# Delta rule: sums of squares of q and k by 32-column ones matmuls and selector matmuls

## The reference, cut to what matters

```python
mixed = jax.nn.silu(conv)
q, k, v = jnp.split(mixed, [KEY_DIM, 2 * KEY_DIM], axis=-1)
...
l2n = lambda t: t / jnp.maximum(jnp.linalg.norm(t, axis=-1, keepdims=True), 1e-12)
q, k = (l2n(q), l2n(k))
...
A = -(jnp.einsum('bhnid,bhnjd->bhnij', k_beta, kc) * decay) * strict
Tm = jax.scipy.linalg.solve_triangular(eye - A, ...)
```

## Time and profile before

| | |
|---|---|
| median of 3 runs | 2497.22 us (2496.21 to 2497.86) |
| span of the profiled execution | 2501.4 us |
| PE busy | 2053.5 us, 82% of the span |
| PE weight loads busy | 1523.0 us, 61% |
| DVE busy | 1579.7 us, 63% |
| ACT busy | 770.9 us, 31% |
| POOL busy | 414.1 us, 17% |
| mean granted PE clock | 0.878 of 2.4 GHz |
| phase c, a round | about 160 us, seven with a successor and one without |

### The profile page before, as it was taken

One profiled execution on the slowest core, in us unless ns is written; L12 is line 12 of the kernel. 1 busy time (PEld: TensorE's weight loads), 2 busy tenths in 40 slices (PEclk: granted clock), 3 DMA queues, 4 the chain that ended last, 5 costly groups with the idle time before them and its releaser, 6 DMA issues. The chain is left out here.

```text
span 2501.4 us, 31043 instructions
## 1 busy us (share of the span) xinstructions
PE 2053.5 (82%) x10850; PEld 1523.0 (61%) x10850; DVE 1579.7 (63%) x3251; ACT 770.9 (31%) x1446; POOL 414.1 (17%) x267
## 2 busy tenths in 40 slices
PE   6988987998956698798887987969879783787786
PEld 5867866554534376485674855838658483455454
DVE  3567564323215776877768677786677864666666
ACT  2334433111113224342243322424334231233233
POOL 1011011000022220322213222123122200110110
PEclk8889888999976899899898998989989895787787
DMA  3000002200010111201212012020120202000000
GB/s 122 5 13 8 4 4 82 101 0 9 0 61 9 42 26 36 51 10 27 51 35 52 9 27 51 21 49 27 27 51 14 55 1 66 7 11 6 13 4 5
DMA packets 128943, 74.51 MB, mean 30 GB/s; under 512 B 106210, under 2 KB 118308, under 8 KB 127812
## 3 DMA queue, kind: packets, MB, share of 16 engines
q1 hardware_dynamic: 128804, 72.67, 11.2%
HBM read 55.69 MB, written 16.78 MB: 29 GB/s over the span
## 5 line engine op out<-in xcount | busy, mean ns | idle before, releaser
L1596 DVE TENSOR_TENSOR c_Y<-c_V,c_bank 128x512 f32<-128x512 f32 x192 | 131.9, 687 | 82.2 <-PE c_bank L1287 82.2
L1287 PE MATMUL c_bank<-c_Y,c_NP 128*128 128x128 f32 x1536 | 176.4, 276 | 0.0
L1287 PEld LDWEIGHTS c_bank<-c_Y,c_NP 128*128 128x128 f32 x1536 | 173.9, 192 | 3.3 <-issue 3.3
L1132 POOL TENSOR_TENSOR c_cv<-c_pad,c_wcv 128x1024 f32<-128x1024 f32 x32 | 72.8, 2274 | 592.9 <-ACT c_pad L1414 411.5
L1220 PE MATMUL c_bank<-c_xT,c_wv 128*128 128x512 f32 x256 | 126.8, 659 | 35.8 <-issue 34.5
L1531 DVE SCALAR_TENSOR_TENSOR c_cv<-c_pad,c_wcqk,c_cv 128x1024 f32<-128x1024 f32 x96 | 143.5, 1503 | 10.8 <-POOL c_cv L1132 10.0
L1269 PE MATMUL c_bank<-c_ident,c_cv 128*128 128x128 f32 x256 | 49.0, 353 | 117.9 <-ACT c_cv L1420 117.9
L1570 DVE SCALAR_TENSOR_TENSOR c_NP<-c_NP,c_cj,c_bank 128x256 f32<-128x256 f32 x256 | 104.9, 476 | 61.5 <-ACT c_NP L1440 61.5
L1531 DVE SCALAR_TENSOR_TENSOR c_cv<-c_pad,c_wcv,c_cv 128x1024 f32<-128x1024 f32 x96 | 134.6, 1410 | 8.0 <-POOL c_cv L1132 4.7
L1582 DVE TENSOR_TENSOR c_tmp<-c_A,c_T 128x31 f32<-128x31 f32 (+15 forms) x248 | 130.0, 524 | 15.1 <-DMA c_A<-diagonal_blocks 6.1
L1220 PE MATMUL c_bank<-c_xT,c_wqk 128*128 128x512 f32 x256 | 129.0, 652 | 5.7 <-ACT c_pad L1414 3.7
(11 more groups left out here) (412 smaller groups left out, 4499.6 us busy)
## 6 DMA issues: line engine op xcount, KB each, us to landing
b_wup<-b_in_wup SPq DMA_DIRECT2D x4, 1280.0 KB, 13.6
c_wqk<-c_in_wqk SPq DMA_DIRECT2D x9, 512.0 KB, 3.5
c_wv<-c_in_wv SPq DMA_DIRECT2D x8, 512.0 KB, 3.4
c_wz<-c_in_wz SPq DMA_DIRECT2D x8, 512.0 KB, 4.9
c_wout<-c_in_wout SPq DMA_DIRECT2D x8, 512.0 KB, 4.6
diagonal_blocks<-c_NP SPq DMA_DIRECT2D x64, 64.0 KB, 2.0
c_A<-diagonal_blocks SPq DMA_DIRECT2D x8, 512.0 KB, 3.2
diagonal_blocks<-c_T SPq DMA_DIRECT2D x8, 512.0 KB
```

Source lines behind the costliest of these rows:

```text
L1132: pool.tensor_tensor(cv[:, m % 2], pad[:, m % 2, :, 0:S], along(w.broadcast_to([P, B]), S), ALU.mult)\
L1287: last = pe.matmul(banks[n % 4][:, b * P:(b + 1) * P], lhsT(h, 4 * q + b), rhs(h, 4 * q + b), start=True, stop=True)
L1596: dve.tensor_tensor(rr(Y, h, q), rr(V, h, q), four(banks[n % 4][:, :]), ALU.subtract).then_inc(s["y_ready"], 1)
```

## The change

The squares are summed the other way round. The stationary operand is now a block of 32 columns of ones, and the squares are the moving one, 512 tokens at a time. Four such matmuls (two chunks e by two halves q of the sequences) write to four groups of 32 partitions of bank 7: each group holds the sums as a row, 32 times over (`sums_of(r, k)`, one call for each key head). ACT copies the bank into `sums`, a view of `A` (`copy_sums`). Eight matmuls with a 128x128 block of `sums` as the stationary operand and the new constant `pick` (128x4, a one at partition 32n of column n) as the moving one turn the rows back into columns of bank 7 (`norms(r)`), and `take_root` takes the root in two instructions, one for each key head.

In PE's list `sums_of(i + 1, 0)` stands between `apply(i, 2)` and the W stage, and `sums_of(i + 1, 1)` and `norms(i + 1)` behind the C stage; nothing stands ahead of `apply(i, 2)` or between W and C any more. In ACT's list `copy_sums(i + 1, 0)` stands ahead of W copy 4, with a wait for `A_out`, and `copy_sums(i + 1, 1)` ahead of `take_root`. `square` waits for `sums_ps` in place of `norms_ps`. Left out of the diff is the list of semaphore names, which gains `sums_ps` and `sums_ready`.

```diff
@@ -968,7 +968,8 @@
         tri = sb("tri", [P, P])
         hidden = sb("hidden", [P, P])
         hiddenb = sb("hiddenb", [P, P], BF16)
-        ones = sb("ones", [P, 1])
+        ones = sb("ones", [P, BL])
+        pick = sb("pick", [P, NBL])
         zero = sb("zero", [P, 1])
         wba = sb("wba", [P, DC, 2 * VAL_HEADS])
         bias = sb("bias", [P, 2, VAL_HEADS])
@@ -997,6 +998,7 @@
         NP = sb("NP", [P, HB, B, 2, S])
         A = sb("A", [P, BL, BL])
         sm = A[:, :, :].rearrange("p a b -> p (a b)").rearrange("p (k b h) -> p k b h", k=4, b=B)
+        sums = A[:, :, :].rearrange("p a b -> p (a b)").rearrange("p (k b n) -> p k b n", k=KB, b=4)
         T = sb("T", [P, BL, BL])
         T0 = sb("T0", [P, BL, BL], BF16)
         tmp = sb("tmp", [P, 256])
@@ -1117,6 +1119,9 @@
             link(pool.memset(Tb[:, :, :], 0.0))
             link(pool.memset(TbT[:, :, :], 0.0))
             link(pool.memset(pad[:, :, :, :], 0.0))
+            link(pool.memset(pick[:, :], 0.0))
+            link(pool.affine_select(out=pick[:, :], in_=pick[:, :], compare_op=ALU.not_equal, fill=1.0, base=0,
+                                    pattern=[[-BL, NBL]], channel_multiplier=1))
             pool.memset(ones[:, :], 1.0).then_inc(s["consts"], 1)
 
             def tap0(r, m, first=False):
@@ -1135,7 +1140,7 @@
             def square(r, m, first=False):
                 pool.wait_ge(s["silu_ready"], at(r, CHUNKS, m + 1))
                 if m >= 2 or not first:
-                    pool.wait_ge(s["norms_ps"], at(r, QK, m - 1))
+                    pool.wait_ge(s["sums_ps"], at(r, KB, m // 2))
                 src = qkT[:, m // 2, m % 2]
                 pool.tensor_tensor(sq[:, m % 2], src, src, ALU.mult).then_inc(s["sq_ready"], 1)
 
@@ -1221,13 +1226,26 @@
                                          start=c == 0, stop=c == DC - 1)
                 last.then_inc(s["proj_ready"], 1)
 
-            def norms(r, m):
-
-                if m == 0:
+            def sums_of(r, k):
+
+                if k == 0:
                     pe.wait_ge(s["pad_ready"], at(r, 2 * CHUNKS, 2))
-                pe.wait_ge(s["sq_ready"], at(r, QK, m + 1))
-                for b in range(B):
-                    last = pe.matmul(banks[7][:, m * B + b:m * B + b + 1], sq[:, m % 2, b, :], ones[:, :], start=True, stop=True)
+                else:
+                    pe.wait_ge(s["sums_ready"], at(r, KB, k))
+                pe.wait_ge(s["sq_ready"], at(r, QK, 2 * k + 2))
+                for e in range(2):
+                    for q in range(2):
+                        rows = slice(BL * (2 * e + q), BL * (2 * e + q) + BL)
+                        last = pe.matmul(four(banks[7][rows, :]), ones[:, :], sq[:, e, 4 * q:4 * q + 4, :], start=True, stop=True)
+                last.then_inc(s["sums_ps"], 1)
+
+            def norms(r):
+
+                pe.wait_ge(s["sums_ready"], at(r, KB, KB))
+                for k in range(KB):
+                    for b in range(4):
+                        n = 4 * k + b
+                        last = pe.matmul(banks[7][:, n * NBL:(n + 1) * NBL], sums[:, k, b, :], pick[:, :], start=True, stop=True)
                 last.then_inc(s["norms_ps"], 1)
 
             def gcrow(i, n):
@@ -1249,7 +1267,7 @@
                 k, b0 = u // 4, 2 * (u % 4)
                 bank = banks[6 + u % 2]
                 if u == 0:
-                    pe.wait_ge(s["root_ready"], at(i, 1, 1))
+                    pe.wait_ge(s["root_ready"], at(i, KB, KB))
                 if u >= 2:
                     pe.wait_ge(s["NP_ready"], at(i, ITEMS, 4 * (u - 1)))
                 for b in range(2):
@@ -1334,18 +1352,15 @@
                 apply(i, 1)
                 if more:
                     project(i + 1, 3)
-                    norms(i + 1, 0)
                 apply(i, 2)
                 if more:
-                    norms(i + 1, 1)
+                    sums_of(i + 1, 0)
                 pe.wait_ge(s["TbT_placed"], at(i, 16 * NBL, 16 * NBL))
                 for n in range(8):
                     pe.wait_ge(s["y_ready"], at(i, 24, 16 + max(n + 1, min(n + 5, 8))))
                     if n >= 4:
                         pe.wait_ge(s["W_ready"], at(i, 8, n - 3))
                     items("W_ps", n, lambda h, b: TbT[:, h * B + b, :], lambda h, b: Y[:, h, b, :])
-                if more:
-                    norms(i + 1, 2)
                 for n in range(8):
                     pe.wait_ge(s["W_ready"], at(i, 8, min(n + 5, 8)))
                     if n >= 4:
@@ -1354,7 +1369,8 @@
                 pe.wait_ge(s["wout_ready"], at(i, 1, 1))
                 pe.wait_ge(s["C_ready"], at(i, 8, 8))
                 if more:
-                    norms(i + 1, 3)
+                    sums_of(i + 1, 1)
+                    norms(i + 1)
                     for n in range(AHEAD + 2):
                         decays_and_grams(i + 1, n)
                 for b in range(B + 1):
@@ -1380,8 +1396,9 @@
             pe.wait_ge(s["gate_step"], 8)
             for m in range(QK):
                 project(0, m, first=True)
-            for m in range(QK):
-                norms(0, m)
+            for k in range(KB):
+                sums_of(0, k)
+            norms(0)
             for n in range(8):
                 decays_and_grams(0, n)
             with pe.Fori(0, ROUNDS - 1) as i:
@@ -1419,10 +1436,18 @@
                 dst = qkT[:, m // 2, m % 2] if m < QK else cv[:, m % 2]
                 act.activation(dst, cv[:, m % 2], ACT.Silu).then_inc(s["silu_ready"], 1)
 
+            def copy_sums(r, k):
+                act.wait_ge(s["sums_ps"], at(r, KB, k + 1))
+                if k == 0:
+                    act.wait_ge(s["gate_step"], 8)
+                act.activation(sums[:, k], four(banks[7][:, :]), ACT.Copy).then_inc(s["sums_ready"], 1)
+
             def take_root(r):
-                act.wait_ge(s["norms_ps"], at(r, QK, QK))
-                act.activation(root[:, :, :, :].rearrange("p k q b -> p (k q b)"), banks[7][:, 0:QK * B], ACT.Sqrt)\
-                    .then_inc(s["root_ready"], 1)
+                act.wait_ge(s["norms_ps"], r + 1)
+                for k in range(KB):
+                    act.activation(root[:, k].rearrange("p e (q b) -> p b e q", q=2),
+                                   banks[7][:, 4 * NBL * k:4 * NBL * (k + 1)].rearrange("p (b e q) -> p b e q", b=4, e=2), ACT.Sqrt)\
+                        .then_inc(s["root_ready"], 1)
 
             def out_gate(i, b):
                 act.wait_ge(s["z_ps"], at(i, B, b + 1))
@@ -1462,6 +1487,9 @@
                         copy_in(i + 1, m + 1)
                         silu(i + 1, m)
                 for n, (h, q) in enumerate(quads):
+                    if more and n == 4:
+                        act.wait_ge(s["A_out"], at(i, 16, 16))
+                        copy_sums(i + 1, 0)
                     if more and n == 5:
                         silu(i + 1, 3)
                     copy_quad(i, "W_ps", n, rr(Y, h, q), "W_ready")
@@ -1471,6 +1499,7 @@
                         act.wait_ge(s["C_ready"], at(i, 8, n + 1))
                         act.activation(rr(V, h, q), rr(Y, h, q), ACT.Square).then_inc(s["csqa_ready"], 1)
                 if more:
+                    copy_sums(i + 1, 1)
                     take_root(i + 1)
                 act.wait_ge(s["var_ready"], at(i, 2, 2))
                 act.activation(f[:, 1], f[:, 0], ACT.Sqrt).then_inc(s["rms_ready"], 1)
@@ -1490,6 +1519,8 @@
                     copy_in(0, m, first=True)
                 if m >= 1:
                     silu(0, m - 1)
+            for k in range(KB):
+                copy_sums(0, k)
             take_root(0)
             for n in range(8):
                 decays(0, n)
@@ -1549,7 +1580,7 @@
             def factors(r):
 
                 link = Linked(dve, s["norm_step"], 3 + KB, r)
-                dve.wait_ge(s["root_ready"], at(r, 1, 1))
+                dve.wait_ge(s["root_ready"], at(r, KB, KB))
                 link(dve.tensor_scalar(nrm[:, 0], root[:, :, :, :], TINY, None, ALU.max))
                 link(dve.reciprocal(nrm[:, 1], nrm[:, 0]))
                 link(dve.tensor_tensor(nrm[:, 2], nrm[:, 1], nrm[:, 1], ALU.mult))
```

More of the change, by code:

```diff
@@ L1013, in layer1_delta_rule @@
         names = """blocks_out T_out A_out weights consts pool_step x_loaded xT_ps xT_copied ba_ps gate_step gate_act gc_ps gates_ready
-            qk_loaded v_loaded z_loaded out_loaded gates_used proj_ready pad_ready tap0_ready conv_step cv_ready silu_ready sq_ready norms_ps
+            qk_loaded v_loaded z_loaded out_loaded gates_used proj_ready pad_ready tap0_ready conv_step cv_ready silu_ready sq_ready sums_ps sums_ready norms_ps
             root_ready rms_ready csqa_ready norm_step gcrow_ps E_ready GP_ps NP_ready gathered elim_step Tb_placed TbT_placed diag_cleared
```

## The result

The change makes the kernel slower, by a little more than its measurement is uncertain. The changed kernel takes 2504.63 us in the median of 15 runs (2496.90 to 2513.26); the kernel before took 2497.08 on the same chips (15 runs, 2494.46 to 2502.30). The ratio is 1.0029 (95% interval 1.0017 to 1.0041), that is +7.5 us. The profiled execution spans 2508.3 us against 2501.4; it is one of the longer runs, timed at 2510.11. The time lies inside the predicted range of 2493 to 2516, 4.6 us above the forecast of 2500; that the change would stay within 0.2% of the kernel before, which the prediction held likeliest, did not come true.

The account below looks back on a forecast made before the run. No engine alone was the limit: DVE sets the first 50 us of a round, then PE, then PE, ACT and DVE hand over work. Seven rounds at 0.0 plus 3.1 us at the phase's start gave 2500 us, range 2493 to 2516.

Parts of the forecast that it names:

- within 0.2% of the kernel before: Whole kernel: a time no more than 5 us from the kernel before, given a chance of 0.48.
- S: Time of one `sums_of` on PE: 0.86 us with four groups at once, plus 0.17 tail and 0.15 shape change, 1.2 us.
- (a): Rival on `sums_of`: column groups overlap only in part, in five steps, S 2.5 us; 2512 us in all, chance 0.20.
- (b): Rival on `sums_of`: column groups don't overlap, S 3.7 us; 2522 us in all, chance 0.10.
- The sentence on 2.38 times for three tiles: Skill's speedup for three column tiles; scaled to four, `sums_of` takes 1.08 instead of 0.86 us, 1.5 us in all.
- The 0.15 for changing the array's shape: Part of the time of one `sums_of`: 0.15 us for the change of tiling, judged from phase a's trace.
- The middle steps: Apply 2 to C: apply 2 starts 1.70 us earlier, C's second item gains 2.4, the last C copy 2.3.
- silu(3) the gate: W to C: silu(3), 1.70 us earlier, and the W copies behind it set C's second item, which gains 2.4 us.
- rival (c): Middle of the round: PE's own time decides, not conv(3) or silu(3); 3.4 us saved a round, 2476 us, chance 0.08.
- The end of a round: Last C copy to roots: sums 1.2, copy 0.65, 0.24 to PE and second root 0.19 add 2.3 us.
- The start of the phase: Before the first round, PE at half clock: sums about 2.0 us, 3.1 us added with no gain against it.
- the balance of a round is 0.0, times 7: Each of seven rounds: 2.3 us gained in the middle against 2.3 added at the end, net 0.0 us.

Follow-up runs that it names:

- experiment 3: The changed kernel with the first `sums_of` of each round issued three times, same results: 2504.30 us, ratio 1.0033 to the kernel before.
- experiment 5: The kernel of experiment 4 with silu(3) on ACT moved behind W copies 5 and 6: 2481.02 us, ratio 0.9925 to the kernel before.
- experiment 12: Also h4_start_cols: the version of experiment 5 with the old one-column norms and one root before the first round: 2478.62 us, ratio 0.9926 to the kernel before.
- f1_fill: The changed kernel with seven unread bf16 matmuls over 512 columns in PE's two waits behind C: 2493.09 us, ratio 0.998 to the kernel before.
- experiment 6: The kernel before with one-column norms 0 and 1 moved behind apply 2, 2 and 3 behind C: 2526.62 us, ratio 1.0103.
- experiment 8: The kernel of experiment 6 with 128 moving columns of ones instead of one: 2489.92 us, ratio 0.9965 to the kernel before.
- experiment 4: The changed kernel with second sums and their copy inside C, norms right behind C ahead of its wait: 2485.05 us, ratio 0.9948 to the kernel before.

## Why the prediction was right and wrong

- **S, the price of one `sums_of`**: 1.2 us taken; eight records last 1.07, and 1.13 pass to the start of the copy. Rivals (a) and (b) are excluded by the starts of the records, 0.45 us apart in fours. The sentence on 2.38 times for three tiles would have made it 1.5 us dearer over the rounds, 1.08 us instead of 0.86. The trace gives two steps of 0.45, 0.90 us, or 3.8 times as fast as the 3.44 of one after another, and 1.00 to the start of W. The 0.15 for changing the array's shape could not be read from the earlier trace rows, where the 16 records behind the change of shape take 3.35 us and the next 16 of the same kind 1.89, so that the first ran at half the pace; here at most 0.14 is left for it.
- **The middle steps**: apply 2 1.70 earlier, W 2.40 (forecast 2.2), C's second item 2.58 (2.4), the last C copy 2.56 (2.3), silu(3) the gate with the W copies right behind it. Experiments 3 and 5 show that gate from both sides, so rival (c) is excluded too: PE's own time was not the limit, by at least the 1.7 us that experiment 3 added.
- **The end of a round**: added 2.3 forecast. From the last C copy's end to the start of the last root the prediction's terms make 4.5 us and the trace has 4.17: the norms start 0.05 us behind the copy's end and not 0.24, and the second root adds 0.08 and not 0.19. With the 0.26 more gained before it, the decays come 0.7 us earlier instead of at the same place; of that 0.4 to 0.5 reach the next round. The table load is hidden, as forecast.
- **The start of the phase**: +3.1 forecast and +3.1 at the root; only +1.6 at the first round's start, 3.0 in the version of experiment 12.
- **The step that failed** is "Against the gain of 2.3 the balance of a round is 0.0, times 7". It priced each of seven rounds at full clock. The prediction read the half clock at the start of the phase and priced it there, but took the granted clock at the end of the rounds as given, though the kernel before fell there in three of seven rounds. The change puts a wait of 0.96 us, 1.07 us of sums, a wait of 0.71 us and 16 records with four moving columns in a row, and the clock fell in five of seven rounds, mostly for twice as long. By the stretches above four long falls and a short one make some 14.4 us, which is the difference to f1_fill, and the three short ones before make 5.4. Against these +9 stands a gain at full clock of 0.4 to 0.5 us a round, 3 in all: together the +6 of the two profiles. The term that was missing is the price of the falls, and it turned a small gain into +7.5 us. It also goes with the scatter: the runs of the change span 16 us, those before 8. In the three shortest of its 15 runs (2496.90 to 2500.01 us) the mean granted clock is 0.876 to 0.879, in the three longest (2511.00 to 2513.26) 0.873 to 0.874. At which place the clock fell in them is not on record.
- That the falls cause the loss is shown by two edits of the changed kernel that leave the chain as it is and change the clock: filled waits (-11.5 us) and 128 moving columns in the selectors (-11.2). Experiments 6 and 8 show the same in the old form, where one column or 128 decides over 35 us. What each of the two, narrow operand and wait, contributes in one round stays open; in the profiles the filled waits end the falls, and the wide selectors leave 10.2 us of half clock where there were 30.7.
- Landing inside the range was in part luck: the falls were not among the rivals, and +7.5 us lies between the forecast and rival (a), which the trace excludes.
- The change's idea gains more when its sums and norms stand inside C, under copies that PE would wait for anyway: 12.4 us in experiment 4. The 19 us of experiment 12 have two other parts, silu(3) moved and the old norms at the start. The kernel before was not run with silu(3) moved, so how much of that it would have gained by itself is open.

## What to carry to other kernels

Matmuls with few moving columns and a fresh load of weights each are worth trying with a wider operand: here 128 columns instead of 1 took the same time on TensorE, its clock held, and that one edit of the kernel before gave 7 us where the change lost 7.5. When a sum of durations comes out near zero, count the rounds in which the granted clock already falls at the place that is changed, and price a chain of short matmuls and short waits there at both clocks. And a new chain of engine to engine steps is better placed inside a stage (here C) than behind its last copy.

## What the runs showed of the hardware

- 32 records with 1 or 16 moving columns, back to back on a busy PE, came with falls of the granted clock to 0.50 in every round (2526.6 and 2521.5 us); with 128 columns at the same pace there was none at these places (2489.9).
- Four float32 matmuls of 512 columns in four column groups run at once: eight records in 1.07 us, where one after another they last 3.60 (1242.94, above). The change of the array's shape costs 0.14 us at most: W starts 1.00 us behind the sums (1253.61 to 1254.61), and 8 x 0.43 / 4 = 0.86 of that is the records.
- PE's idle time at the turn of the loop, ahead of the value projection, is 5.76 us in the kernel before, by nothing that the profile shows, and 1.07 in the changed one, with a wait that has a name. PE's timeline of the kernel before:

```profile
1315.36 1.19 PE L1220 MATMUL c_bank<-c_xT,c_wv 128*128 128x512 f32 x1 [5.76 <-issue]
```

of the changed one:

```profile
1314.79 1.52 PE L1225 MATMUL c_bank<-c_xT,c_wv 128*128 128x512 f32 x3 [1.07 <-DVE c_acc L1655]
```

and the queue that loads instructions, on the page of the changed kernel (86 packets and 1.41 MB before):

```profile
q8 instruction: 32, 0.52, 0.1%
```

The two go together in all kernels run: those built on the change have 31 or 32 packets apart from h4_start_cols, which has 86 as the kernel before, and those with `norms` in the old form 68 to 86. The clock goes with it as well: in the kernel before it falls for 3.41 or 6.83 us at each of the six turns, in the changed one at none. Yet no time was gained by it: VectorE's own idle at the turn is the same (24.9 and 25.2 us in all), and h4_start_cols, with a fall at every turn, has rounds as short as experiment 5 without one (156.8 to 157.2 us against 156.8 to 157.3, the first and last apart). Why the instructions are loaded less often is open.
